# Gated attention kernel: another order of the first chunks' layers and loads, and separate buffers for x and attention

## Chip, core and metric

The kernel runs on one NeuronCore of a Trainium2 chip. The metric is the device time of one launch in microseconds (us), median of several runs. A profiled execution gives a span and a trace of every engine: TensorE (PE, matmuls; its weight loads are PEld), VectorE (DVE), ScalarE (ACT), GpSimd (POOL), and SyncE (SP), which only issues DMAs here.

## The reference

x and ctx are (4, 512, 512) in float32, H = 16 heads of HD = 32. What is computed:

```python
Q = layernorm(x) @ Wq.T + bq; K = ctx @ Wk.T + bk; V = ctx @ Wv.T + bv   # each as (b, s, 16, 32)
score = einsum('bshd,bsgd->bshg', Q, K)          # per token: 16 heads against 16 heads
attn = einsum('bshg,bsgd->bshd', softmax(score), V).reshape(b, s, 512)
x = x + tanh(g_xattn) * (attn @ Wo.T + bo)
x = x + tanh(g_ffn) * (layernorm(x) @ (Wf * scale[:, None]).T + bf)
```

The attention is inside a token: each token has a 16 x 16 matrix of scores between its heads.

## The kernel before, in words

The 2048 tokens are worked through in 8 chunks of 256 tokens (two tiles of 128). A chunk goes through these stages, named as in the text:

- **K, V** (from the chunk's context, loaded transposed by `load_ctx`), **Q** (from the normalised x, turned on TensorE by `turn_x1`): dense layers, 512 x 512.
- **score**: the queries and keys are brought to another layout by way of DRAM (`save_q`, `load_q`, `save_k`, `load_k`, then `lay_keys` on ScalarE), and 64 small matmuls give the scores, in two banks.
- softmax on VectorE (`scores_turn`, `softmax_a`, `softmax_b`) with the exponential on ScalarE (`exp`); then the weights are spread into a larger tile by VectorE (`spread_first`) and GpSimd (`spread_last`).
- **attend**: 64 small matmuls against V (reloaded by `load_v`), copied out by ScalarE (`attn_copy`).
- **O** (attention times Wo), residual, second layernorm, turning (`turn_x2`), **F** (times Wf), residual, output.

Every dense layer splits both operands into a high and a low part (float32r) and runs three products: high x high, high x low, low x high. High parts are made by ScalarE (`high`, line 541), low parts by VectorE (`low`, line 675), and for the context by GpSimd (`ctx_low`, line 927). This holds for the weights too, which are loaded and split piece by piece at the start (`load_w`, `w_high`, `w_low`; `W_ORDER` in line 180 sets the order that the counting semaphores `w_hi` and `w_lo` assume). K, Q, V and O, F share two PSUM banks, acc0 and acc1: a layer may write a bank when the layer before has been read out of it (`bank_free`). K and Q are written two 128-column blocks a bank ("block 0" and "block 1" are the banks).

Each engine has its own instruction stream, written out by hand. First a prologue (SP lines 303 to 332, TensorE 491 to 500, ScalarE 624 to 637, VectorE 811 to 830, GpSimd 953 to 972), then a step function that is called for chunk 0 and 1, in a hardware loop for 2 and on, and again for the last ones. An engine runs its stream strictly in order, and waits at semaphores for others. On TensorE a step i before is: score(i), O(i-1), K(i+1), Q(i+1), attend(i), turn x2(i-1), V(i+1), F(i-1), turn x1(i+2). In the prologue it is K0 with x0's turning in its middle, Q0, V0, turning of x1, and 6 warming matmuls (`keep_clock`, whose counts are in `WARM`).

Some orders matter in the prediction. The raw W_f and W_v are loaded into the tile `late`, into which `attn_copy` writes the attention as well, so the first copy waits for W_f's low parts (line 599). The raw W_k, W_q and W_o are loaded into the `spread` tile. In the prologue GpSimd runs root(0, 1), the inverse standard deviation of chunk 1's x, and behind it ctx_low(1). VectorE makes the statistics for it in norm_stats(0, x_norm, 1), line 823, and waits in `w_low` for the high part of the piece. The high parts of x1 and of the attention share the tile `xa_parts`. `tanh_g`, made by ScalarE in step 0, waits for all five constants (`consts_in`), as do VectorE's `scale_w` calls.

## Time and profile before

| | us |
|---|---|
| median of 3 runs | 323.98 (323.53 to 325.38) |
| profiled execution, its own time | 322.51 |
| its span | 320.8 |
| TensorE busy | 292.4 (91%) |
| VectorE busy | 216.5 (67%) |
| ScalarE busy | 141.3 (44%) |
| GpSimd busy | 107.3 (33%) |
| mean granted TensorE clock | 0.968 of full |

The chain of waits that ended last spends 61% of the span in TensorE, 13% in DMAs, 10% in VectorE and 8% in SyncE's queue. A row of a timeline gives the start in us from the span's start, the duration, the engine and source line, output and inputs by tile, and in brackets how long the engine had been idle and what released it. Rows of several instructions are merged, so that the duration holds small waits. The granted clock is 1.0 at 2.4 GHz and 0.5 at 1.2 GHz.

### The profile page before, as it was taken

To read this page: it belongs to the slowest core of one execution; us is meant where nothing else is said; L and a number is where in the kernel's file an instruction comes from. 1 tells how busy PE (TensorE), PEld (TensorE's weight loads), DVE (VectorE), ACT (ScalarE), POOL (GpSimd) and SP (SyncE) were. 2 spreads that over 40 slices of the span, in tenths; PEclk is the share of its full clock that TensorE was granted. 3 is DMA by queue.
4 is the path that set the end of the run, shared out by engine and by line. 5 is a ranking of instruction groups with operands and counts; after the bars stand their busy time and mean duration, and the time that the engine had idled before them with its cause. 6 is when DMAs were issued, how large, how long until landed. Compare 5 with 4: busy or idle time off the path is not lost.

```text
span 320.8 us, 6628 instructions
## 1 busy us (share of the span) xinstructions
PE 292.4 (91%) x2562; PEld 258.9 (81%) x2562; DVE 216.5 (67%) x321; ACT 141.3 (44%) x277; POOL 107.3 (33%) x83
## 2 busy tenths in 40 slices
PE   6499699759998999999999999999999997894895
PEld 6498699548986899889988898889988996774684
DVE  3857479835876696568774887568746953497463
ACT  4355424572377033923385236803592239304500
POOL 3500215520445133533173126214433342042422
PEclk9869899959999999999999999999999999799999
DMA  7966688473543735364543556184436226512001
GB/s 224 332 225 212 218 227 264 137 190 85 188 151 118 191 133 195 115 149 140 176 142 135 127 196 190 71 196 153 174 131 134 66 87 183 127 66 67 33 33 67
DMA packets 64596, 48.52 MB, mean 151 GB/s; under 512 B 35776, under 2 KB 53952, under 8 KB 64576
## 3 DMA queue, kind: packets, MB, share of 16 engines
q1 hardware_dynamic: 64576, 48.25, 49.0%
q8 instruction: 13, 0.21, 0.3%
q14 instruction: 7, 0.06, 0.1%
HBM read 31.46 MB, written 16.78 MB: 150 GB/s over the span
## 4 chain that ended last, share of the span: by engine, by line
PE 61%; DMA 13%; DVE 10%; SPq 8%; issue 4%; ACT 3%; POOL 1%; DVEq 0%; POOLq 0%
PE acc L377 48%; PE score_ps L463 6%; DMA k_scratch<-k_t 6%; PE turn_ps L406 4%; DMA q_scratch<-q_t 3%; PE attn_ps L478 3%; DVE spread L786 3%; SPq L230 2%; DMA x_norm<-x 2%; DMA q_pad<-q_scratch 2%; ACT late L602 2%; SPq L271 2%; DVE x_norm L711 2%; DVE stats L689 2%; SPq L256 1%
## 5 line engine op out<-in xcount | busy, mean ns | idle before, releaser
L602 ACT ACTIVATE late<-attn_ps 32x256 f32<-32x256 f32 x128 | 48.1, 376 | 24.9 <-PE attn_ps L478 18.2
L946 POOL TENSOR_TENSOR spread<-probs_t,same_token 128x1536 f32<-128x1536 f32 (+1 forms) x8 | 26.2, 3278 | 75.2 <-DVE probs_t L778 75.2
L377 PEld LDWEIGHTS acc<-ctx_parts,wk_parts 128*128 128x128 f32 x384 | 48.9, 199 | 1.9 <-issue 1.4
L377 PE MATMUL acc<-ctx_parts,wk_parts 128*128 128x256 f32 x384 | 49.6, 290 | 0.8 <-DVE wk_parts L675 0.8
L377 PE MATMUL acc<-wf_parts,x_parts 128*128 128x512 f32 (+1 forms) x192 | 44.7, 387 | 3.0 <-ACT x_parts L541 1.6
L377 PE MATMUL acc<-xa_parts,wq_parts 128*128 128x256 f32 x384 | 47.4, 283 | 0.0
L377 PE MATMUL acc<-wo_parts,xa_parts 128*128 128x512 f32 x192 | 46.1, 395 | 0.8 <-ACT xa_parts L541 0.8
L377 PEld LDWEIGHTS acc<-xa_parts,wq_parts 128*128 128x128 f32 x384 | 46.7, 192 | 0.0
L377 PE MATMUL acc<-wv_parts,ctx_parts 128*128 128x512 f32 x192 | 45.7, 393 | 0.0
L377 PEld LDWEIGHTS acc<-wo_parts,xa_parts 128*128 128x128 f32 x192 | 35.7, 189 | 10.2 <-issue 1.7
L377 PEld LDWEIGHTS acc<-wf_parts,x_parts 128*128 128x128 f32 x192 | 34.7, 188 | 11.1 <-ACT x_parts L541 2.4
L921 POOL TENSOR_TENSOR rstd<-var_eps,minus_half 128x1 f32<-128x1 f32 (+1 forms) x24 | 15.2, 634 | 85.0 <-DVE var_eps L700 85.0
L377 PEld LDWEIGHTS acc<-wv_parts,ctx_parts 128*128 128x128 f32 x192 | 35.5, 188 | 7.3 <-issue 0.2
L927 POOL TENSOR_TENSOR ctx_parts<-ctx_raw,ctx_parts 128x1024 fp32r<-128x1024 f32 (+1 forms) x8 | 18.7, 2340 | 44.7 <-ACT ctx_parts L541 44.7
L463 PE MATMUL score_ps<-q_pad,k_keys 128*32 128x128 f32 x512 | 23.3, 348 | 10.7 <-DMA q_pad<-q_scratch 7.5
L786 DVE TENSOR_TENSOR spread<-probs_t,same_token 128x2560 f32<-128x2560 f32 (+1 forms) x8 | 32.4, 4048 | 0.0
L463 PEld LDWEIGHTS score_ps<-q_pad,k_keys 128*32 128x32 f32 x512 | 19.7, 133 | 13.0 <-DMA q_pad<-q_scratch 7.9
L576 ACT ACTIVATE q_t<-acc,bq_col 128x256 f32<-128x256 f32 x32 | 13.5, 472 | 30.6 <-PE acc L377 30.5
L711 DVE TENSOR_SCALAR x_norm<-x_norm,moments,rstd 128x512 f32<-128x512 f32 x16 | 22.7, 1461 | 6.2 <-POOL rstd L921 6.2
L569 ACT ACTIVATE probs<-probs 128x512 f32<-128x512 f32 x8 | 5.1, 633 | 49.5 <-DVE probs L763 49.5
L576 ACT ACTIVATE k_t<-acc,bk_col 128x256 f32<-128x256 f32 x32 | 13.4, 471 | 28.4 <-PE acc L377 28.4
L748 DVE STREAM_TRANSPOSE turned<-score_ps 128x512 f32<-128x512 f32 x16 | 11.5, 719 | 20.1 <-PE score_ps L463 20.1
(62 smaller groups left out, 352.9 us busy)
## 6 DMA issues: line engine op xcount, KB each, us to landing
ctx_raw<-ctx_t SPq DMA_DIRECT2D x8, 512.0 KB, 4.4
x_norm<-x SPq DMA_DIRECT2D x8, 512.0 KB, 6.0
k_scratch<-k_t SPq DMA_DIRECT2D x8, 512.0 KB, 3.5
k_rows<-k_scratch SPq DMA_DIRECT2D x32, 128.0 KB, 2.9
q_scratch<-q_t SPq DMA_DIRECT2D x8, 512.0 KB, 3.4
q_pad<-q_scratch SPq DMA_DIRECT2D x32, 128.0 KB, 2.8
v_scratch<-v_or_norm SPq DMA_DIRECT2D x8, 512.0 KB, 2.8
v_keys<-v_scratch SPq DMA_DIRECT2D x8, 512.0 KB, 4.8
```

The source lines that it names most:

```text
L377: last = pe.matmul(dst, left(a, k), right(b, k), start=(n == 0), stop=(n == len(terms) - 1))
L406: last = pe.transpose(turn_ps[t][:, P * k:P * (k + 1)], src[:, t, P * k:P * (k + 1)], ident[:])
L463: last = pe.matmul(score_ps[b][HD * pair:HD * (pair + 1), P * o:P * (o + 1)], k_keys[:, 2 * n:2 * n + 2].rearrange("p s g -> p (s g)"), q_ ...
L478: last = pe.matmul(attn_ps[HD * t:HD * (t + 1), P * eight:P * (eight + 1)], v_keys[:, GT // OCT * t + eight, :], spread[:, GROUPS // TILES ...
L576: nc.scalar.activation(dst[:, :, m, :], acc[m // 2][:, TOK * (m % 2):TOK * (m % 2 + 1)].rearrange("p (t n) -> p t n", t=GROUPS), ACT.Ident ...
L602: nc.scalar.activation(attn_t[HD * q:HD * (q + 1), :, GT * t:GT * (t + 1)] .rearrange("p m (o e) -> p m o e", e=OCT), attn_ps[HD * t:HD * ...
L711: nc.vector.tensor_scalar(dst[:, t, :], src[:, t, :], moments[which][:, t, 0:1], rstd[which][:, t:t + 1], ALU.subtract, ALU.mult).then_inc ...
L748: nc.vector.transpose(flat[:, BANK * b:BANK * (b + 1)].rearrange("p (e s x) -> p e s x", s=2, x=HT), score_ps[b][:].rearrange("p (e x s) - ...
L786: nc.vector.tensor_tensor(spread[:, :n].rearrange("p o h t -> p (o h) t"), probs_t[:, :n].rearrange("p o h -> p (o h)").unsqueeze(2).broad ...
L921: nc.gpsimd.tensor_tensor(rstd[which][:, t], var_eps[which][:, t], minus_half[:, t], ALU.pow).then_inc(n_rstd[which], count)
L927: nc.gpsimd.tensor_tensor(ctx_parts[:, LO, k], ctx_raw[:, k], ctx_parts[:, HI, k].bitcast(F32), ALU.subtract).then_inc(ctx_lo, 1)
L946: nc.gpsimd.tensor_tensor(spread[:, first:].rearrange("p o h t -> p (o h) t"), probs_t[:, first:].rearrange("p o h -> p (o h)").unsqueeze( ...
```

## The change

The x parts and the attention parts get a tile each, `x1_parts` and `at_parts`, so that their writers wait for their own readers only. The order of layers on TensorE becomes K0, V0 (x0's turning in its middle), Q0, K1, turning of x1, block 0 of Q1; in step 0 score 0, block 1 of Q1, V1, attend 0; in step 1 score 1, K2, O0, Q2, attend 1 and on as before. From step 2 on it is the old order. The order of the weights becomes K, V, Q, O, F, and SyncE, ScalarE and VectorE follow the new order. GpSimd clears `q_pad` ahead of its first root and leaves all of context 0's low part to VectorE. First uses of a weight wait for its high part at the start of the product and for its low part only where it is read; the order of the mixed products is turned round where that postpones the wait. The 6 warming matmuls go.

```diff
-WARM = (12, 6, 0, 2, 4, 3)
+WARM = (12, 0, 2, 4, 3)
...
-        xa_parts = sb("xa_parts", [P, 2, KC, TOK], F32R)
+        x1_parts = sb("x1_parts", [P, 2, KC, TOK], F32R)
+        at_parts = sb("at_parts", [P, 2, KC, TOK], F32R)
...
-        W_ORDER = [("wk", wk_t, 0, (0, P, D // 2)), ("wq", wq_t, 1, (0, D // 2)), ("wv", wv_t, 2, (0, D // 2)),
+        W_ORDER = [("wk", wk_t, 0, (0, P, D // 2)), ("wv", wv_t, 2, (0, D // 2)), ("wq", wq_t, 1, (0, D // 2)),
                    ("wo", wo_t, 0, (0, D // 2)), ("wf", wf_t, 2, (0, D // 2))]
-        WK, WQ, WV, WO, WF = range(len(W_ORDER))
...
             load_ctx(0)
-            load_w(WK, 0)
-            load_w(WK, 1)
+            for j in range(3):
+                load_w(WK, j)
             load_x(0)
-            load_w(WK, 2)
+            for j in range(2):
+                load_w(WV, j)
             for col, dram in ((bk_col, bk), (bq_col, bq)):
                 sp.dma_start(col[:], dram).then_inc(biases_in, DMA)
-            for n in (WQ, WV):
-                for j in range(2):
-                    load_w(n, j)
             sp.dma_start(bv_row[:], bv.partition_broadcast(P)).then_inc(bv_in, DMA)
+            for j in range(2):
+                load_w(WQ, j)
+            load_ctx(1)
+            save_k(0)
             load_x(1)
-            load_ctx(1)
+            load_k(0)
             load_w(WO, 0)
+            save_v(0)
             load_w(WO, 1)
-            save_k(0)
-            load_k(0)
             save_q(0)
             sp.wait_ge(zeroed, 1)
             load_q(0)
-            save_v(0)
+            save_k(1)
+            load_v(0)
             load_w(WF, 0)
             load_w(WF, 1)
             sp.dma_start(scale_row[:], scale.partition_broadcast(P)).then_inc(consts_in, DMA)
             for n_gate, dram in enumerate((g_attn, g_ffn)):
                 sp.dma_start(gates[:, n_gate:n_gate + 1], dram.partition_broadcast(P)).then_inc(consts_in, DMA)
+            load_k(1)
             for row, dram in ((bo_row, bo), (bf_row, bf)):
...
                 if exists(i + 1):
-                    save_k(i + 1)
-                    load_k(i + 1)
+                    if not first(i):
+                        save_k(i + 1)
+                        load_k(i + 1)
                     save_q(i + 1)
                     load_q(i + 1)
                 if exists(i + 1):
...
-
-                terms = [(k, a, b) for a, b in ((HI, HI), (HI, LO), (LO, HI)) for k in range(KC)]
+            def product(dst, left, right, low_ready=None, right_low_ready=None, right_low_last=False):
+
+                mixed = ((LO, HI), (HI, LO)) if right_low_last else ((HI, LO), (LO, HI))
+                terms = [(k, a, b) for a, b in ((HI, HI), *mixed) for k in range(KC)]
                 for n, (k, a, b) in enumerate(terms):
                     if low_ready and (k, a) == (0, LO):
                         low_ready()
...
-                                (lambda: low_ready(t)) if low_ready and n == 0 else None).then_inc(done, 1)
-
-            def cols_layer(w, parts, done, prev, prev_c, w_new=None, between=None):
-
-                for b in range(2):
+                                (lambda: low_ready(t)) if low_ready and n == 0 else None,
+                                w_low_ready if t == 0 else None, bool(w_low_ready)).then_inc(done, 1)
+
+            def cols_layer(w, parts, done, prev, prev_c, w_new=None, low_ready=None, blocks=range(2)):
+
+                for b in blocks:
                     bank_free(prev, prev_c, b)
                     for m in (2 * b, 2 * b + 1):
-                        if between and m == 2:
-                            between()
+                        w_low_ready = None
                         if w_new is not None and P * m in W_ORDER[w_new][3]:
-                            pe.wait_ge(w_lo, pieces_to(w_new, W_ORDER[w_new][3].index(P * m)))
+                            ready = pieces_to(w_new, W_ORDER[w_new][3].index(P * m))
+                            pe.wait_ge(w_hi, ready)
+
+                            def w_low_ready(ready=ready):
+                                pe.wait_ge(w_lo, ready)
                         last = product(acc[b][:, TOK * (m % 2):TOK * (m % 2 + 1)],
                                        lambda a, k: weights[w][:, a, k, P * m:P * (m + 1)],
-                                       lambda c, k: parts[:, c, k, :])
+                                       lambda c, k: parts[:, c, k, :],
+                                       w_low_ready, low_ready if m == 0 else None)
                     last.then_inc(done, 1)
...
-                rows_layer(ctx_parts, "wv", v_mm, lambda t: bank_free("q", c, t))
-
-            def q_layer(c, w_new=None):
-                pe.wait_ge(x1_lo, TILES * (c + 1))
-                cols_layer("wq", xa_parts, q_mm, "k", c, w_new)
-
-            def k_layer(c, prev, prev_c, w_new=None, between=None):
-                pe.wait_ge(ctx_lo, c + 1)
-                cols_layer("wk", ctx_parts, k_mm, prev, prev_c, w_new, between)
+            def v_layer(c, prev="q", t_done=None):
+                def high_ready(t):
+                    if t_done and t == 1:
+                        t_done()
+                    bank_free(prev, c, t)
+                    if first(c) and t == 0:
+                        pe.wait_ge(w_hi, pieces_to(WV, 1))
+                rows_layer(ctx_parts, "wv", v_mm, high_ready,
+                           w_low_ready=(lambda: pe.wait_ge(w_lo, pieces_to(WV, 1))) if first(c) else None)
+
+            def q_layer(c, prev="k", prev_c=None, w_new=None, blocks=range(2)):
+                if 0 in blocks:
+                    pe.wait_ge(x1_lo, TILES * (c + 1))
+                cols_layer("wq", x1_parts, q_mm, prev, c if prev_c is None else prev_c, w_new, blocks=blocks)
+
+            def k_layer(c, prev, prev_c):
+                if first(c):
...
+                    cols_layer("wk", ctx_parts, k_mm, prev, prev_c)
             def o_layer(c, prev, prev_c):
                 def high_ready(t):
                     pe.wait_ge(at_hi, TILES * c + t + 1)
                     bank_free(prev, prev_c, t)
-                rows_layer(xa_parts, "wo", o_mm, high_ready, lambda t: pe.wait_ge(at_lo, TILES * c + t + 1))
+                rows_layer(at_parts, "wo", o_mm, high_ready, lambda t: pe.wait_ge(at_lo, TILES * c + t + 1))
...
             keep_clock(WARM[0])
-            pe.wait_ge(ctx0_lo, 1)
-            k_layer(0, None, 0, w_new=WK, between=lambda: turn_x1(0, lambda t: None))
-            q_layer(0, w_new=WQ)
-            pe.wait_ge(w_lo, pieces_to(WV, 1))
-            v_layer(0)
+            k_layer(0, None, 0)
+            v_layer(0, "k", lambda: turn_x1(0, lambda t: None))
+            q_layer(0, "v", 0, WQ)
+            k_layer(1, "q", 0)
             turn_x1(1, x1_read(0))
-
-            keep_clock(WARM[1])
+            q_layer(1, blocks=(0,))
             def tensor_step(i):
...
                     f_layer(i - 2, "v", i)
-                if exists(i - 1):
-                    if not exists(i - 2):
-                        pe.wait_ge(w_lo, pieces_to(WO, 1))
-                    o_layer(i - 1, *(("f", i - 2) if exists(i - 2) else ("v", i)))
-                if exists(i + 1):
-                    k_layer(i + 1, *(("o", i - 1) if exists(i - 1) else ("v", i)))
-                    q_layer(i + 1)
+                if first(i):
+                    q_layer(1, blocks=(1,))
+                    v_layer(1)
+                elif first(i - 1):
+                    k_layer(2, "v", 1)
+                    pe.wait_ge(w_lo, pieces_to(WO, 1))
+                    o_layer(0, "k", 2)
+                    q_layer(2, "o", 0)
+                else:
+                    if exists(i - 1):
+                        o_layer(i - 1, "f", i - 2)
+                    if exists(i + 1):
+                        k_layer(i + 1, "o", i - 1)
+                        q_layer(i + 1)
                 if exists(i):
                     attend(i)
...
                         f_layer(i - 1, "v", i + 1)
                 else:
+                    keep_clock(WARM[2 * (i - CHUNKS) + 3])
+                    turn_x2(i - 1, x2_read(i - 2), (0,))
                     keep_clock(WARM[2 * (i - CHUNKS) + 4])
-                    turn_x2(i - 1, x2_read(i - 2), (0,))
-                    keep_clock(WARM[2 * (i - CHUNKS) + 5])
                     f_layer(i - 1, "o", i - 1, lambda: turn_x2(i - 1, x2_read(i - 2), (1,)))
...
                 def free():
-                    if exists(c - 2):
-                        act.wait_ge(o_mm, TILES * (c - 1))
-                    else:
-                        reached(act, q_mm, 2 * c)
-                turned_hi(xa_parts, x1_turned, x1_hi, c, free)
+                    reached(act, q_mm, 2 * c)
+                turned_hi(x1_parts, x1_turned, x1_hi, c, free)
             def x2_high(c):
                 turned_hi(x2_parts, x2_turned, x2_hi, c, lambda: reached(act, f_mm, TILES * c))
...
                 if tile == 0:
-                    act.wait_ge(q_mm, 2 * (c + 2) if exists(c + 1) else 2 * CHUNKS)
+                    reached(act, o_mm, TILES * c)
                 act.wait_ge(a_out, MOVES * c + MOVES // TILES * (tile + 1))
-                high(xa_parts[:, HI, :, P * tile:P * (tile + 1)],
+                high(at_parts[:, HI, :, P * tile:P * (tile + 1)],
                      attn_t[:, :, P * tile:P * (tile + 1)]).then_inc(at_hi, 1)
             def w_high(n, j):
...
             ctx_high(0)
-            for n, j in ((WK, 0), (WK, 1), (WK, 2), (WQ, 0), (WQ, 1)):
+            for n, j in ((WK, 0), (WK, 1), (WK, 2), (WV, 0), (WV, 1)):
                 w_high(n, j)
+            act.wait_ge(biases_in, 2 * DMA)
+            k_bias(0, (0,))
+            w_high(WQ, 0)
+            k_bias(0, (1,))
+            w_high(WQ, 1)
             x1_high(0)
-            act.wait_ge(biases_in, 2 * DMA)
-            k_bias(0)
-            w_high(WV, 0)
-            w_high(WV, 1)
-            q_bias(0)
+            ctx_high(1)
+            q_bias(0, (0,))
             w_high(WO, 0)
+            q_bias(0, (1,))
             w_high(WO, 1)
-            ctx_high(1)
+            lay_keys(0)
+            k_bias(1)
             x1_high(1)
-            lay_keys(0)
+            q_bias(1, (0,))
             def scalar_step(i):
                 if exists(i):
                     exp(i)
-                if exists(i + 1):
-                    if not first(i):
-                        x1_high(i + 1)
+                if exists(i + 1) and not first(i):
+                    x1_high(i + 1)
                     k_bias(i + 1)
                 if first(i):
                     act.wait_ge(consts_in, 5 * DMA)
                     nc.scalar.activation(tanh_g[:], gates[:], ACT.Tanh).then_inc(gates_done, 1)
-                if exists(i + 1):
-                    q_bias(i + 1)
                 if first(i):
+                    q_bias(1, (1,))
+                    lay_keys(1)
                     w_high(WF, 0)
                     w_high(WF, 1)
+                elif exists(i + 1):
+                    q_bias(i + 1)
                 if exists(i):
                     attn_copy(i, 0)
                 if exists(i - 1):
                     x2_high(i - 1)
+                if first(i):
+                    attn_high(i, 0)
                 if exists(i):
                     attn_copy(i, 1)
-                if exists(i + 1):
+                if exists(i + 1) and not first(i):
                     lay_keys(i + 1)
                 if exists(i):
-                    attn_high(i, 0)
+                    if not first(i):
+                        attn_high(i, 0)
                     attn_high(i, 1)
                 if exists(i + 2):
                     ctx_high(i + 2)
...
             dve.wait_ge(ctx_hi, 1)
-            low(ctx_parts[:, LO, :KC // 2], ctx_raw[:, :KC // 2], ctx_parts[:, HI, :KC // 2]).then_inc(ctx0_lo, 1)
-            w_low(WK, 0)
-            w_low(WK, 1)
+            low(ctx_parts[:, LO], ctx_raw[:], ctx_parts[:, HI]).then_inc(ctx_lo, 1)
+            for j in range(3):
+                w_low(WK, j)
             norm_stats(0, x_norm, 0)
-            norm_apply(0, x_norm, x_norm, 0)
-            w_low(WK, 2)
-            w_low(WQ, 0)
-            turned_lo(xa_parts, x1_hi, x1_lo, 0)
-            w_low(WQ, 1)
             w_low(WV, 0)
             w_low(WV, 1)
+            norm_apply(0, x_norm, x_norm, 0)
+            w_low(WQ, 0)
+            dve.wait_ge(bv_in, DMA)
+            v_bias(0, 0)
+            w_low(WQ, 1)
+            turned_lo(x1_parts, x1_hi, x1_lo, 0)
+            v_bias(0, 1)
+            w_low(WO, 0)
             norm_stats(0, x_norm, 1)
             norm_apply(0, x_norm, x_norm, 1)
-            dve.wait_ge(bv_in, DMA)
-            v_bias(0, 0)
-            w_low(WO, 0)
             w_low(WO, 1)
-            v_bias(0, 1)
-            turned_lo(xa_parts, x1_hi, x1_lo, 1)
+            turned_lo(x1_parts, x1_hi, x1_lo, 1)
             def vector_step(i):
                 if final(i - 1):
                     return last_step(i)
                 scores_turn(i)
-                if first(i - 1):
-                    o_residual(i - 1, 0)
                 softmax_a(i)
                 if final(i):
                     return last_softmax_step(i)
-                if first(i - 1):
-                    o_residual(i - 1, 1)
-                elif exists(i - 1):
+                if exists(i - 1) and not first(i - 1):
                     o_residual(i - 1, 0)
                 softmax_b(i)
                 if exists(i - 1) and not first(i - 1):
                     o_residual(i - 1, 1)
                 if exists(i + 1) and not first(i):
-                    turned_lo(xa_parts, x1_hi, x1_lo, i + 1)
+                    turned_lo(x1_parts, x1_hi, x1_lo, i + 1)
                 spread_first(i)
+                if first(i - 1):
+                    o_residual(i - 1, 0)
+                    o_residual(i - 1, 1)
                 if first(i):
                     dve.wait_ge(consts_in, 5 * DMA)
                     scale_w(0)
...
             nc.gpsimd.affine_select(out=same_token[:], in_=same_token[:], compare_op=ALU.is_ge, fill=0.0,
                                     base=H - 1, pattern=[[H, OCT]], channel_multiplier=-1).then_inc(consts_made, 1)
-            ctx_low(0, KC // 2)
+            nc.gpsimd.memset(q_pad[:], 0.0).then_inc(zeroed, 1)
             root(0, 0)
-            nc.gpsimd.memset(q_pad[:], 0.0).then_inc(zeroed, 1)
             root(0, 1)
             ctx_low(1)
             pool.wait_ge(w_lo, pieces_to(WO, 1))
```

## Rows read from the trace of the kernel before

**Rows 1.** Windows (stretch, length, busy per engine, clock, DMA share, GB/s): a loop step.

```profile
104.55:138.89 34.34, 34.34 (x315) 30.55 (x313) 24.25 (x38) 16.23 (x33) 10.81 (x10) 1.00 0.48 149
```

**Rows 2.** The chain that ended last (start, us, what).

```profile
17.28 4.55 PE acc L377 x24
...
22.78 4.92 DMA k_scratch<-k_t
...
105.42 2.46 PE score_ps L463 x60
107.88 17.18 PE acc L377 x120
```

**Rows 3.** Timeline of TensorE: start, duration, operation, idle before and its releaser.

```profile
15.31 1.97 PE L406 MATMUL turn_ps<-ident,x_norm 128*128 128x128 f32 x8 [4.28 <-DVE x_norm L711]
...
27.41 5.63 PE L377 MATMUL acc<-wv_parts,ctx_parts 128*128 128x512 f32 x24
...
37.81 3.55 PE L463 MATMUL score_ps<-q_pad,k_keys 128*32 128x128 f32 x64 [2.55 <-DMA q_pad<-q_scratch]
...
68.06 3.64 PE L463 MATMUL score_ps<-q_pad,k_keys 128*32 128x128 f32 x64 [4.97 <-DMA q_pad<-q_scratch]
71.63 5.99 PE L377 MATMUL acc<-wo_parts,xa_parts 128*128 128x512 f32 x24
...
98.84 5.71 PE L377 MATMUL acc<-wf_parts,x_parts 128*128 128x512 f32 x24 [1.34 <-DVE v_or_norm L742]
```

**Rows 4.** Timeline of VectorE, 0 to 60 us.

```profile
25.95 1.28 DVE L689 BATCH_NORM_STATS2 stats<-x_norm 128x6 f32<-128x512 f32 x2
...
41.41 0.72 DVE L748 STREAM_TRANSPOSE turned<-score_ps 128x512 f32<-128x512 f32 x1 [0.99 <-PE score_ps L463]
...
49.60 5.01 DVE L727 TENSOR_TENSOR late<-late,scale_row 128x1024 f32<-128x1024 f32 x2
...
57.19 2.35 DVE L675 TENSOR_TENSOR wf_parts<-late,wf_parts 128x1024 fp32r<-128x1024 f32 x2
```

**Rows 5.** Timeline of ScalarE, 0 to 70 us.

```profile
11.51 1.06 ACT L541 ACTIVATE wq_parts<-spread 128x1024 fp32r<-128x1024 f32 x1 [0.42 <-DMA spread<-wq_t]
12.87 1.06 ACT L541 ACTIVATE wq_parts<-spread 128x1024 fp32r<-128x1024 f32 x1 [0.31 <-DMA spread<-wq_t]
...
21.85 0.84 ACT L576 ACTIVATE k_t<-acc,bk_col 128x256 f32<-128x256 f32 x2 [3.21 <-PE acc L377]
...
59.63 6.37 ACT L602 ACTIVATE late<-attn_ps 32x256 f32<-32x256 f32 x16 [3.74 <-DVE wf_parts L675]
66.03 1.93 ACT L590 ACTIVATE k_keys<-k_rows 128x1024 f32<-128x1024 f32 x1
```

**Rows 6.** Timeline of GpSimd, 0 to 75 us.

```profile
28.05 0.70 POOL L921 TENSOR_TENSOR rstd<-var_eps,minus_half 128x2 f32<-128x2 f32 x1 [13.07 <-DVE var_eps L700]
...
70.06 2.39 POOL L927 TENSOR_TENSOR ctx_parts<-ctx_raw,ctx_parts 128x1024 fp32r<-128x1024 f32 x1 [7.97 <-ACT ctx_parts L541]
```

**Rows 7.** The page's DMA issues: count, size of one, median us to landing.

```profile
ctx_raw<-ctx_t SPq DMA_DIRECT2D x8, 512.0 KB, 4.4
...
k_scratch<-k_t SPq DMA_DIRECT2D x8, 512.0 KB, 3.5
...
spread<-wo_t SPq DMA_DIRECT2D x2, 512.0 KB, 6.9
```

**Rows 8.** Timeline of SyncE: issues and how long each held it.

```profile
27.78 1.76 SPq L271 DMA_DIRECT2D k_rows<-k_scratch  x4
...
41.17 7.26 SPq L230 DMA_DIRECT2D x_norm<-x  x1
...
69.10 3.48 SPq L230 DMA_DIRECT2D x_norm<-x  x1
```

**Rows 9.** Windows of one us; the clock stands third from the end.

```profile
20.00:21.00 1.00, 1.00 (x7) 1.00 (x6) 0.31 (x1) 0.00 (x0) 0.00 (x0) 0.52 1.02 363
...
72.00:73.00 1.00, 1.00 (x5) 0.79 (x5) 0.47 (x1) 0.00 (x0) 0.45 (x1) 0.92 0.62 97
```

39 lines of the change are left out of this document (20 added, 19 removed).

## The prediction

> **What bounds the kernel now.** I read the stretches of the windows first: from the third chunk on TensorE is busy for 34.34 of each 34.34 us at full granted clock [rows 1], so a change that leaves the loop's work alone can only gain or lose ahead of it. The chain that ended last says the same: the layers of a loop step follow each other without a gap, three of them in 17.18 us (5.73 each) and the scores in 2.46 [rows 2]. The change moves nothing across the loop's start: by the loop's first score both kernels have done the same matmuls but for 6 warming ones. What counts is therefore at what time the last layer ahead of the loop, F of chunk 0, starts. Before, that is 98.84 us, after a 1.34 us wait [rows 3].
>
> Then I asked what set TensorE's pace up to there. It waits 2.55 us for the padded queries before score 0 (37.81), 4.97 us before score 1 (68.06), and runs from O0 (71.63) to the end of V2 (98.84 - 1.34 = 97.50) practically without a stop, 25.87 us [rows 3]. Behind score 0 lies a chain outside TensorE, which is the backbone of what follows: VectorE's last transpose of score 0 starts at 41.41, its low parts of W_f end at 59.54 (57.19 + 2.35) [rows 4]; ScalarE's copies of attention 0 wait for just that (59.63 to 66.00), then it lays the keys of chunk 1 (1.93) [rows 5]; at last GpSimd makes the low part of context 2, ending at 72.45 [rows 6]. From 41.41 to 72.45 are 31.04 us, and K2 needs its end. Before, O0 stands ahead of K2 and covers the last of it.
>
> **The change, part by part, in order of time.**
>
> *K0, V0, Q0.* K0 needs the high part of W_k first and its low part later, so it runs behind the loads. The second piece of W_v stands in the load order where the second piece of W_q stood, and that was converted from 12.87 on [rows 5]: V's high part is there at 13.9, the first half of K0's bias (0.84) at 14.8. V0 with x's turning (5.73 and about 1) ends at 21.5, Q0 at 27.3. Before, Q0 and V0 together were done at 33.0 [rows 3]. The clearing of q_pad, moved ahead of GpSimd's first root, costs nothing, since GpSimd waits there for VectorE. That is a lead of some 5 us, and the question is who takes it back.
>
> *K1.* K1 waits for context 1's low part. On GpSimd this stands behind the root of chunk 1's x (`root(0, 1)`, then `ctx_low(1)`); the root waits for VectorE's statistics of chunk 1; and the new order of VectorE puts these behind the low part of W_o's first piece. That piece is loaded by a queue entry that was moved behind the saving and reloading of K0. Before, it was issued before K was saved, and the statistics stood ahead of it. So a layer of chunk 1 now hangs on a weight of the O layer. The chain:
> - W_q's first piece: 512 + 512 + 256 KB more stand ahead of it than before, at 1.36 us per 512 KB (11.51 to 12.87) [rows 5], 3.4 us: 14.9. High part 1.06, second half of K0's bias 0.84 [rows 5]: 16.8.
> - K0's saving. It took 4.92 with more in the queue [rows 2]; a 512 KB load has a median of 4.4 [rows 7], K's saving one of 3.5. I take 4.4, ends 3.5 and 4.92: 21.2.
> - Four reloads are issued in 1.76 [rows 8]: 23.0.
> - W_o's first piece: median 4.4 for a context load, 6.9 for W_o before, where all came at once [rows 7]. Few bytes stand ahead of it now, so 4.4: 27.5.
> - High 1.06, low 1.18 (half of 2.35) [rows 4, 5]: 29.7.
> - Statistics up to the root's start, 25.95 to 28.05, and the root, 0.70 [rows 4, 6]: 32.5.
> - Low part of context 1, 2.39 [rows 6]: 35.0 with the gaps.
>
> So K1 starts at 35.0 instead of 27.3: TensorE stands for 7.7 us. For the last item, GpSimd and VectorE are released by the same root. The rows have GpSimd starting its next instruction at once after a root, so I take 2.39 undelayed. The Trainium skill (SBUF — State Buffer, "SBUF: two separate sides") says that the two share one port pair as an exclusive lock and that the first to start holds it; if the normalising of x came first, context 1 would be up to 1.0 us later, and so would the sum.
>
> *The clock.* Before, after waits of 4.28, 2.55 and 4.97 us TensorE came back at 1.2 GHz: from 15.31 to 21.0, from 37.81 to 41.4 and from 68.06 to 72.1 [rows 3, 9]. The granted clock is 0.52 in the 21st us, and 0.92 in the 73rd, so full from 72.2. The half of K0 that ran at 1.2 GHz for 3.7 of its us took 4.55 instead of 2.87, which is 0.45 us lost per us [rows 2]. K1 after 7.7 us of waiting then loses 4.1 x 0.45 = 1.85, ends 1.6 and 2.6. The Trainium skill (TensorE: Matmul & The Clock Gate, "Terms") puts the loss at half the slow time; that would be 2.05, and the sum 0.4 higher for two layers. The waits of some 2 us before V0 and before Q1 I cost at nothing, nearest to the 1.34 one [rows 3] after which no slow stretch followed; 1.85 each if wrong.
>
> *Up to score 0.* K1 ends at 35.0 + 5.73 + 1.85 = 42.6. Second half of its bias 0.84, high part of x 1.06 (as many values as W_q's piece), low part of its second half 0.6 (half of 1.18), 0.3 of gaps [rows 4, 5]: 45.4. Half of Q1, 2.87: score 0 starts at 48.3 and ends at 50.8, its queries having long landed. VectorE's last transpose starts at 50.8 instead of 41.41: 9.4 us late.
>
> *The backbone.* Its work is unchanged but that the keys of chunk 1 are laid earlier, out of it: 31.04 - 1.93 = 29.1. K2 can start at 50.8 + 29.1 = 79.9. The second half of Q1, V1, attend 0 and the turning fill only part of it; these 11 or 12 us cover nothing that ends later. Score 1 runs in the gap, some 7 us ahead of that, and a gap of 3.7 us is left, so K2 too starts at 1.2 GHz: 1.85, low end 0. Then K2, O0, Q2, attend 1, turning, V2: 25.87 less the 0.2 that O0 lost before, plus 1.85, gives 107.4 for F0's start. Its own wait of 1.34 goes, because O0's residuals, which it hung on, come earlier relative to V2.
>
> *The rest.* Own buffers for x1 and attention let ScalarE take x's high part earlier in each step; TensorE has no gap there that could shrink [rows 1]: nothing. The later order of the product's terms changes no count: nothing. Loads of V, W_f and constants now stand behind K1's saving. The next issue after the V reload was held for 7.26 or 3.48 us [rows 8]. From 43.5 with 3.5 I get the last constant issued at 52.3 and landed by 58 to 60; VectorE wants it at 59: nothing, 4 if the hold is 7.3.
>
> **Sum.** 107.4 - 98.84 = 8.6 us. The profiled execution took 322.51 us, so 331.1; it lies 1.5 below the median of the runs, 323.98, to which I add the same: 332.6, forecast 332.5. Low ends (saving 0.9 less, clock 0.25 and 1.85 less, some 3 in all): 329.5. High ends (W_o 2.5 more, saving 0.5, clock 0.8 twice, port 1.0): 338.
>
> **Rivals.**
> - *K1 doesn't wait.* W_o's piece would have to be there 7.5 us before 27.3, at 19.8. By the rows K0's save is not even back then. If so all the same, score 0 ends near 41.7, K2 can start near 71.0, and F0 starts at 98.5 if K2 is slow, 96.7 if not: 323.6 or 321.8. The second is faster by 0.7%, and decides from K2's clock. For it: every other part of the change takes a wait away. Together 0.14, 0.07 of each.
> - *The constants bind.* If the V reload holds the queue for the 7.26 of before, bo and bf land near 63, W_f's scaling starts 4 us late, and all of it reaches K2: 336.5. Against it: the 7.26 came with W_f and the constants queued ahead, which they aren't now. 0.12.
> - *The backbone is shorter.* The scaling of W_f took 5.01 us for two pieces whose low parts took 2.35 [rows 4], GpSimd's share of the spread beside it. Without that the backbone would lose 2.7: 329.8. Against it: the spread stays on both engines. 0.10.
> - *A smaller wait at K1 that the chain takes up, other small gains:* 324 to 326, 0.04.
>
> **How the numbers follow.** My forecast has 0.60. Rows carry each link, but the start is made of many. The range from 325.5 to 337.5 takes in the forecast's ends but for the last 0.5, the constants and the shorter backbone; left out are the first rival and the far tails, some 0.17. About 0.5% (1.6 us) is what a measurement of this kernel can tell from no change. Slower 0.84 (forecast, constants, backbone and half the last), same 0.09 (the first rival with a slow K2, and half the last), faster 0.07 (the first rival with a fast K2).
>
> **What would show it.** K1's first matmul should start at 34 to 37 us, released by GpSimd's low part of context 1, which follows the root directly; W_o's high part should be released by its DMA at 27 to 28. The granted clock should be at 1.2 GHz in K1. Score 0 ends near 51, VectorE's low W_f near 69, K2 starts near 80 released by GpSimd, with 3 to 4 us of wait, and F0 near 107 with none. The loop's period should stay at 34.34. If K1 starts before 30, the forecast is wrong at its root; if K1 is late and K2 isn't, the backbone was not what I took it for.

## The result, and the profile after

The changed kernel is slower: 334.11 us median of 4 runs (333.88 to 337.1) against 324.68 of the kernel before, a ratio of 1.034 (95% interval 1.027 to 1.041), and the medians lie 9.4 us apart. Ratios and intervals, here and below, are taken from the runs outside a slower state in which some executions fall, so they are not the quotients of the medians, which here would be 1.029. The profiled execution took 334.08 us with a span of 332.3.

From the page after (busy time and share of the span; K's layer with its idle time and what ended it):

```profile
PE 294.8 (89%) x2550; PEld 259.8 (78%) x2550; DVE 214.1 (64%) x321; ACT 141.5 (43%) x277; POOL 106.3 (32%) x82
...
L381 PE MATMUL acc<-ctx_parts,wk_parts 128*128 128x256 f32 x384 | 52.6, 300 | 13.5 <-POOL ctx_parts L956 13.1
```

TensorE's work is the same, 294.8 us against 292.4. K's layers waited 13.5 us, 13.1 of them for GpSimd's low parts of the context, a wait that the page before doesn't have. The chain that ended last (start, us, what) shows the first of these waits from its source:

```profile
17.21 2.99 DMA k_scratch<-k_t
...
20.27 0.34 SPq L269
...
22.08 6.28 DMA spread<-wo_t
28.38 1.06 ACT wo_parts L567
29.47 1.23 DVE wo_parts L707
30.69 1.21 DVE stats L721 x2
...
32.69 0.70 POOL rstd L951
33.39 2.32 POOL ctx_parts L956
...
35.75 7.56 PE acc L381 x48
...
54.00 7.38 DMA bf_row<-bf
...
78.65 2.35 POOL ctx_parts L956
...
81.05 19.85 PE acc L381 x120
```

K0's saving starts at 17.21 and its reloads at 20.27. Only then, at 22.08, is W_o's first piece asked for. From there one thing follows the other: high part, low part, statistics of chunk 1, root, low part of context 1, K1 at 35.75. The constants (54.00), and behind them the low part of context 2 (78.65), lead to K2 at 81.05. Between VectorE's low parts of W_f and that last low part stands ScalarE, with the copies of attention 0 and the high part of context 2, which GpSimd waited for:

```profile
69.89 3.16 ACT L626 ACTIVATE late<-attn_ps 32x256 f32<-32x256 f32 x8 [3.73 <-DVE wf_parts L707]
...
77.53 1.04 ACT L567 ACTIVATE ctx_parts<-ctx_raw 128x1024 fp32r<-128x1024 f32 x1
```

TensorE's timeline, with the idle time ahead of a group and its releaser:

```profile
20.99 5.91 PE L381 MATMUL acc<-x_parts,wq_parts 128*128 128x256 f32 x48
35.75 7.55 PE L381 MATMUL acc<-ctx_parts,wk_parts 128*128 128x256 f32 x48 [8.86 <-POOL ctx_parts L956]
...
46.04 3.13 PE L381 MATMUL acc<-x_parts,wq_parts 128*128 128x256 f32 x24 [1.87 <-DVE x_parts L707]
49.11 2.52 PE L484 MATMUL score_ps<-q_pad,k_keys 128*32 128x128 f32 x64
...
81.05 8.63 PE L381 MATMUL acc<-ctx_parts,wk_parts 128*128 128x256 f32 x48 [4.21 <-POOL ctx_parts L956]
...
109.11 5.61 PE L381 MATMUL acc<-wf_parts,x_parts 128*128 128x512 f32 x24
```

Q0 ends at 26.9, where before V0 ended at 33.0 [rows 3]: the lead of 6 us is there. K1 then waits 8.86 us and score 0 starts at 49.11 instead of 37.81. K2 waits 4.21 us, and F0 starts at 109.11 instead of 98.84, 10.27 us later. VectorE's rows for the same stretch:

```profile
33.43 3.01 DVE L743 TENSOR_SCALAR x_norm<-x_norm,moments,rstd 128x512 f32<-128x512 f32 x2 [0.88 <-POOL rstd L951]
...
51.69 0.72 DVE L780 STREAM_TRANSPOSE turned<-score_ps 128x512 f32<-128x512 f32 x1 [0.43 <-PE score_ps L484]
...
61.40 3.46 DVE L759 TENSOR_TENSOR late<-late,scale_row 128x1024 f32<-128x1024 f32 x2 [1.45 <-DMA bf_row<-bf]
...
67.45 2.35 DVE L707 TENSOR_TENSOR wf_parts<-late,wf_parts 128x1024 fp32r<-128x1024 f32 x2
```

The clock, in stretches of the changed kernel (granted clock third from the end), beside a loop step:

```profile
39.00:40.00 1.00, 1.00 (x9) 1.00 (x9) 0.00 (x0) 0.00 (x0) 0.00 (x0) 0.88 0.00 0
81.00:87.00 6.00, 5.96 (x28) 5.96 (x29) 5.20 (x9) 2.09 (x4) 2.07 (x1) 0.50 0.28 91
306.00:308.00 2.00, 1.96 (x5) 1.57 (x6) 1.15 (x2) 0.00 (x0) 0.99 (x2) 0.50 0.00 0
114.56:148.90 34.34, 34.34 (x314) 30.55 (x313) 24.26 (x39) 16.24 (x33) 12.41 (x9) 1.00 0.51 154
```

K1 runs at 1.2 GHz until 39.2, K2 until 87, and the loop step takes its 34.34 us as before [rows 1]. Of the 11.5 us between the spans, 10.27 are there when F0 starts. The other 1.2 come in the last chunk: here the clock was low from 306 to 308.9, and the first product of an F layer took 3.43 us where it had been 2.11 before:

```profile
306.04 3.43 PE L381 MATMUL acc<-wf_parts,x_parts 128*128 128x512 f32 x8 [1.64 <-ACT x_parts L567]
```

This is scatter and no effect of the change: after a wait of 1.62 to 1.64 us the same product took 3.68 to 3.78 us in the traces of experiments 6, 8 and 9, and 2.11 or 2.12 in those of the other seven.

### The profile page after: what moved, and what is told of

Same layout as the page of the kernel before. It is cut to its first block, busy times and chain, and to the rows that moved or that the text cites. A ratio compares the mean times of both kernels' runs of the same rounds, so it can differ in the third digit from the quotient of the medians.

```text
span 332.3 us, 6598 instructions
## 1 busy us (share of the span) xinstructions
PE 294.8 (89%) x2550; PEld 259.8 (78%) x2550; DVE 214.1 (64%) x321; ACT 141.5 (43%) x277; POOL 106.3 (32%) x82
## 4 chain that ended last, share of the span: by engine, by line
PE 70%; DMA 7%; DVE 6%; SPq 5%; issue 5%; POOL 3%; ACT 3%; DVEq 0%; POOLq 0%
PE acc L381 57%; PE score_ps L484 5%; PE attn_ps L499 4%; PE turn_ps L415 3%; SPq L299 2%; DMA spread<-wq_t 2%; DMA bf_row<-bf 2%; DMA spread<-wo_t 2%; ACT late L626 2%; POOL ctx_parts L956 1%; DVE stats L721 1%; DVE spread L818 1%; DVE late L759 1%; POOL rstd L951 1%; SPq L269 1%
## 5 line engine op out<-in xcount | busy, mean ns | idle before, releaser
L381 PE MATMUL acc<-ctx_parts,wk_parts 128*128 128x256 f32 x384 | 52.6, 300 | 13.5 <-POOL ctx_parts L956 13.1
L381 PE MATMUL acc<-wv_parts,ctx_parts 128*128 128x512 f32 x192 | 48.2, 406 | 6.2 <-ACT q_t L600 4.9
L381 PE MATMUL acc<-x_parts,wq_parts 128*128 128x256 f32 x384 | 47.7, 283 | 1.9 <-DVE x_parts L707 1.9
L381 PEld LDWEIGHTS acc<-x_parts,wq_parts 128*128 128x128 f32 x384 | 46.8, 192 | 2.5 <-DVE x_parts L707 2.1
L381 PE MATMUL acc<-wo_parts,at_parts 128*128 128x512 f32 x192 | 45.7, 394 | 0.9 <-ACT at_parts L567 0.9
L381 PEld LDWEIGHTS acc<-wo_parts,at_parts 128*128 128x128 f32 x192 | 35.5, 188 | 9.8 <-issue 1.3
L707 DVE TENSOR_TENSOR x_parts<-turn_ps,x_parts 128x512 fp32r<-128x512 f32 x32 | 20.7, 682 | 21.7 <-ACT x_parts L567 21.7
L956 POOL TENSOR_TENSOR ctx_parts<-ctx_raw,ctx_parts 128x1024 fp32r<-128x1024 f32 x7 | 17.0, 2428 | 36.5 <-ACT ctx_parts L567 36.5
L707 DVE TENSOR_TENSOR at_parts<-late,at_parts 128x512 fp32r<-128x512 f32 x16 | 10.5, 688 | 20.9 <-ACT at_parts L567 20.9
L567 ACT ACTIVATE x_parts<-turn_ps 128x512 fp32r<-128x512 f32 x32 | 17.6, 597 | 14.4 <-PE turn_ps L415 14.1
```

Of the source, the lines that this page charges most:

```text
L381: last = pe.matmul(dst, left(a, k), right(b, k), start=(n == 0), stop=(n == len(terms) - 1))
L567: return nc.scalar.activation(dst, src, ACT.Identity)
L707: return nc.vector.tensor_tensor(dst, src, hi.bitcast(F32), ALU.subtract)
L956: nc.gpsimd.tensor_tensor(ctx_parts[:, LO], ctx_raw[:], ctx_parts[:, HI].bitcast(F32), ALU.subtract).then_inc(ctx_lo, 1)
```

## The experiments

In all of them "before" is the kernel before, run on the same chip between them: 322.7 us median for experiments 1, 2, 3 and 5, 323.6 for 4, 6, 7 and 8, 323.0 for 9 and 10. Ratios are to that. A trace shows one execution, and its own time is given where it lies far from the median. The order of V0 and Q0, the later waits for low parts and the missing warming matmuls were not run by themselves.

**1. GpSimd makes context 1's low part ahead of the root.**

```diff
-            root(0, 1)
             ctx_low(1)
+            root(0, 1)
```

> The changed kernel, but GpSimd makes the low part of context 1 ahead of the root of chunk 1's x. Theory (K1 hangs on W_o's first piece by way of that root): context 1's low part is done by 25, K1 starts at 27 with no wait worth naming, its second half at 30.2, score 0 ends near 42.7 instead of 51.5, all behind it moves by the same 8.8 us, so K2 starts near 72.3, F0 near 100.4, and the time is 325.3 against 334.1. Rival (K1's wait was idle time that the chain behind score 0 would have taken anyway, through the constants or the copies of attention): K1 starts at 27 too, but K2 stays after 77 and the time above 330.

Measured: 326.01 us, ratio 1.014 (1.007 to 1.021). TensorE:

```profile
26.31 3.04 PE L381 MATMUL acc<-ctx_parts,wk_parts 128*128 128x256 f32 x24
...
71.63 8.05 PE L381 MATMUL acc<-ctx_parts,wk_parts 128*128 128x256 f32 x48 [4.29 <-POOL ctx_parts L956]
...
99.12 5.61 PE L381 MATMUL acc<-wf_parts,x_parts 128*128 128x512 f32 x24
```

One line gives back 10.0 us of F0's start in the trace and 2% of the time. (The profiled execution took 322.86 us, the least of the four, which go up to 328.19.) K1 starts at 26.31 with no wait; its second half waits 0.22 for ScalarE. The expected 72.3 for K2 and 100.4 for F0 came out at 71.63 and 99.12. K2 still waits 4.29 us. So the wait of K1 is the larger part of the loss, and it isn't slack that the chain behind score 0 would have used.

**2. VectorE makes chunk 1's statistics ahead of W_o's low part.**

```diff
-            w_low(WO, 0)
             norm_stats(0, x_norm, 1)
             norm_apply(0, x_norm, x_norm, 1)
+            w_low(WO, 0)
```

> The changed kernel, but VectorE makes chunk 1's statistics and norm ahead of the low part of W_o's first piece; GpSimd keeps its order. Theory (the link from W_o to the statistics is what delays the root): x of chunk 1 lands near 22.2, root by 25.0, context 1's low part by 27.4, K1 starts at 27.4, and the time is within 0.5 us of the kernel with the context ahead of the root, near 325.5. Rival (it is GpSimd's own order or context 1's high part that delays it, not W_o): K1 starts after 33, and the time stays near 334.

Measured: 325.84 us, 1.013 (1.006 to 1.019); the profiled execution took 323.62.

```profile
27.05 6.02 PE L381 MATMUL acc<-ctx_parts,wk_parts 128*128 128x256 f32 x48 [0.18 <-POOL ctx_parts L956]
...
99.81 5.61 PE L381 MATMUL acc<-wf_parts,x_parts 128*128 128x512 f32 x24
```

The other end of the same link, with the same effect: GpSimd's order alone does no harm if the root isn't kept waiting by W_o. Each cut of the link is enough.

**3. Warming matmuls in the two waits.**

```diff
+            keep_clock(66)
             k_layer(1, "q", 0)
...
+                    pe.wait_ge(v_out, TILES + 1)
+                    keep_clock(30, acc[0])
                     k_layer(2, "v", 1)
```

> The changed kernel with 66 warming matmuls ahead of K1 and 30 ahead of K2 (these into acc0, once V1 has been read out of it), so that neither wait is idle; nothing else moves. Theory (K1 and K2 lose to the 1.2 GHz clock after their waits): K1 takes 5.8 instead of 7.55 us, score 0 ends 1.8 earlier, and so does K2's start; K2 takes 5.8 to 6.0 instead of 8.63, so 2.7 more: 329.6 against 334.1. Rival (the slow layers are covered by the chain outside TensorE, as the queries' reload or the constants): under 1.5 us of gain, above 332.5.

Measured: 336.91 us, 1.047 (1.041 to 1.052), slower than the changed kernel.

```profile
26.80 14.90 PE L510 MATMUL score_ps<-ident 128*128 128x128 f32 x132
41.46 6.00 PE L381 MATMUL acc<-ctx_parts,wk_parts 128*128 128x256 f32 x48
...
88.72 6.00 PE L381 MATMUL acc<-ctx_parts,wk_parts 128*128 128x256 f32 x48
```

A miss, by my counting: the warming matmuls are two instructions each, and 66 take 14.90 us, not 8.3. They held K1 until 41.46 and K2 until 88.72. But both K layers took 6.00 us, near the 5.92 of K in the loop, instead of 7.55 and 8.63. So this run shows the price of the clock, but not what it costs the kernel; for that the fillers have to fit the waits.

**4. The same with 36 and 16.**

```diff
-            keep_clock(66)
+            keep_clock(36)
...
-                    keep_clock(30, acc[0])
+                    keep_clock(16, acc[0])
```

> As the last kernel with warming matmuls, but 36 ahead of K1 and 16 ahead of K2, because one of them takes 0.226 us (14.90 us for 66) and not the 0.125 that I had counted. Theory (the slow clock in K1 and K2 is on the path): K1 still starts at 35.8 and takes 6.0, score 0 ends 1.6 earlier than in the changed kernel, K2 takes 6.0 instead of 8.63, F0 starts 4.2 earlier, near 104.9; 1.021 of the kernel before. Rival (covered by the queue's or VectorE's chain): F0 after 107.5, 1.03 or more.

Measured: 329.61 us, 1.017 (1.009 to 1.026).

```profile
37.03 6.00 PE L381 MATMUL acc<-ctx_parts,wk_parts 128*128 128x256 f32 x48 [0.55 <-POOL ctx_parts L959]
...
80.82 6.02 PE L381 MATMUL acc<-ctx_parts,wk_parts 128*128 128x256 f32 x48 [0.37 <-POOL ctx_parts L959]
...
106.27 5.61 PE L381 MATMUL acc<-wf_parts,x_parts 128*128 128x512 f32 x24
```

The waits stay and only the clock is kept up: K1 and K2 take 6.0 us. In this execution W_o's first piece was asked for 1.4 us later (23.48), so that K1 starts at 37.03, 1.3 later, and F0 at 106.27 instead of the expected 104.9. By the ratios about half of the loss is given back. Between the two traces the spans differ by 4.1 us: 2.8 up to F0, and 1.3 in the last chunk's product, which took 2.12 us here and is scatter. Both layers' slow clock is on the path.

**5. Own buffers alone, in the kernel before.** The x parts and the attention parts get a tile each, and their writers wait only for Q and for O.

```diff
-                    if exists(c - 2):
-                        act.wait_ge(o_mm, TILES * (c - 1))
-                    else:
-                        reached(act, q_mm, 2 * c)
-                turned_hi(xa_parts, x1_turned, x1_hi, c, free)
+                    reached(act, q_mm, 2 * c)
+                turned_hi(x1_parts, x1_turned, x1_hi, c, free)
...
-                    act.wait_ge(q_mm, 2 * (c + 2) if exists(c + 1) else 2 * CHUNKS)
+                    reached(act, o_mm, TILES * c)
```

> The kernel before with one part of the change alone: own buffers for the x parts and the attention parts, and the waits that go with them. Theory (TensorE has no gap in the loop that could shrink): no difference beyond 0.3%, 322.5 to 325.5, loop period 34.34. Rival (the separate buffers free a wait before the loop or in the last chunks): faster by 1 us or more.

Measured: 323.34 us (10 runs), 1.004 (0.999 to 1.008). No difference that can be told from none, and none over 0.8%; the loop's period is 34.34. In this trace score 0 waited 4.07 us for its queries, where it had been 2.55 before, and F0 started at 100.05; whether the edit has a part in that, one trace can't tell.

**6. Context 1 ahead of the root, and O0 ahead of K2 again.** On VectorE the residuals of O0 go back to their places around `softmax_a`.

```diff
-                    k_layer(2, "v", 1)
                     pe.wait_ge(w_lo, pieces_to(WO, 1))
-                    o_layer(0, "k", 2)
-                    q_layer(2, "o", 0)
+                    o_layer(0, "v", 1)
+                    k_layer(2, "o", 0)
+                    q_layer(2)
```

> The changed kernel with context 1's low part ahead of the root, and in step 1 O0 ahead of K2 as before the change (with its residuals placed on VectorE as before). Theory (K2 put ahead of O0 uncovers the wait for context 2, so the second loss sits there): score 1 ends near 67.4 and O0 starts at once on attention that is there at 64 and 69; K2 follows with no wait at full clock; Q2 ends near 84.7 instead of 90.8, then VectorE's chain lets F0 start near 94.7 instead of 99.1; 4.4 us faster than with the context alone, 0.99 to 0.995 of the kernel before. Rival (O0 waits as long for the attention as K2 for the context): F0 stays at 98 to 100.

Measured: 322.21 us (10 runs), 0.993 (0.988 to 0.999): 0.7% faster than the kernel before, and 2 points below experiment 1 (1.014). The profiled execution took 324.31.

```profile
71.11 5.71 PE L381 MATMUL acc<-wo_parts,at_parts 128*128 128x512 f32 x24
76.66 5.92 PE L381 MATMUL acc<-ctx_parts,wk_parts 128*128 128x256 f32 x48
...
98.09 5.73 PE L381 MATMUL acc<-wf_parts,x_parts 128*128 128x512 f32 x24 [1.39 <-DVE v_or_norm L774]
```

O0 follows score 1 with no wait and K2 follows O0 at full clock. So the second loss of the changed kernel is its order of K2 and O0. F0 at 98.09 missed the expected 94.7, because score 0 started at 43.35 instead of 39.66 as in experiment 1: this execution's K1 began 1.8 later, and its Q1 half, at 1.2 GHz, took 4.51 instead of 3.13. From score 0 to F0 it is 54.7 us, against 59.5 in experiment 1: 4.7 us gained, where 4.4 were expected.

**7. O0 ahead of K2 alone:** the changed kernel with the diff of experiment 6, TensorE's and VectorE's, and without that of experiment 1.

> The changed kernel with O0 ahead of K2 alone; K1's wait for the root stays. Theory (the two losses are separate and add up): K1 starts at 35.8 as in the changed kernel, K2 no longer waits, F0 starts near 103.5 instead of 109.1, 5.6 us faster than the changed kernel, 1.017 of the kernel before. Rival (the order of O0 and K2 matters only once K1 is early): F0 after 107.5, 1.03.

Measured: 329.48 us, 1.019 (1.011 to 1.028).

```profile
35.72 8.40 PE L381 MATMUL acc<-ctx_parts,wk_parts 128*128 128x256 f32 x48 [8.67 <-POOL ctx_parts L957]
...
79.30 5.73 PE L381 MATMUL acc<-wo_parts,at_parts 128*128 128x512 f32 x24
...
106.30 5.73 PE L381 MATMUL acc<-wf_parts,x_parts 128*128 128x512 f32 x24 [1.38 <-DVE v_or_norm L774]
```

K1 waits as in the changed kernel, the wait ahead of K2 is gone. F0 missed the expected 103.5 by 2.8 us, again ahead of score 0, which started at 51.38 instead of 49.11: K1 ran at 1.2 GHz until 41.2 and took 8.40, and Q1's half took 4.60. Behind score 0 the gain is 5.1 us, as the theory has it (5.6). From 1.034 this mends 1.5 points and experiment 1 mends 2.0; together (experiment 6) 4.1. Within the intervals the two add up.

**8. Three more mends.** Experiment 6 with the statistics of experiment 2, `lay_keys(0)` behind `x1_high(1)` on ScalarE, and on SyncE the loads of W_f and all constants ahead of `load_k(1)` and `load_v(0)`.

```diff
-            lay_keys(0)
             k_bias(1)
             x1_high(1)
+            lay_keys(0)
...
             save_k(1)
-            load_v(0)
             load_w(WF, 0)
...
-            load_k(1)
             for row, dram in ((bo_row, bo), (bf_row, bf)):
                 sp.dma_start(row[:], dram.partition_broadcast(P)).then_inc(consts_in, DMA)
+            load_k(1)
+            load_v(0)
```

> The kernel with context 1 ahead of the root and O0 ahead of K2, and three things more: chunk 1's statistics ahead of W_o's low part, the laying of chunk 0's keys behind K1's bias and x1's high part, and the loads of W_f and all constants ahead of the reloads of K1 and V0. Expected: score 0 starts near 38.3, the constants land by 47 so that neither the tanh nor the second half of V1 waits, VectorE's low W_f ends near 57.8, F0 starts near 91; 3.5 us faster than the kernel with the first two, 0.98 of the kernel before. Rival (VectorE's chain from score 0 on binds by itself, whatever the loads do): F0 at 94 or later.

Measured: 320.1 us, 0.987 (0.978 to 0.996), 1.3% faster than the kernel before; its interval overlaps that of experiment 6, so what the three add isn't shown by the times.

```profile
35.62 4.28 PE L381 MATMUL acc<-x_parts,wq_parts 128*128 128x256 f32 x24 [1.86 <-DVE x_parts L707]
...
68.15 5.75 PE L381 MATMUL acc<-wo_parts,at_parts 128*128 128x512 f32 x24
...
95.14 5.70 PE L381 MATMUL acc<-wf_parts,x_parts 128*128 128x512 f32 x24 [1.36 <-DVE v_or_norm L774]
```

Score 0 starts at 39.84, not at 38.3: again Q1's half fell to 1.2 GHz (4.28 us). F0 starts at 95.14, not at 91, after 1.36 us of waiting for VectorE; nobody waits for the constants any more, but W_f's low parts end at 60.77 instead of the expected 57.8. The rival that I had named holds: from score 0 on the chain that ended last runs through VectorE and through layers that wait for it, and from score 0 to F0 it is 55.3 us, no less than in experiment 6. Against the kernel before, score 0 starts 2.0 us later and F0 3.7 earlier: there score 1 waited 4.97 us for its queries and started at 68.06 [rows 3], here it starts at 64.69 without that wait.

**9. With 7 warming matmuls ahead of Q1's first half.**

```diff
+            keep_clock(7)
             q_layer(1, blocks=(0,))
```

> The mended kernel with 7 warming matmuls (1.58 us) in the 1.87 us wait ahead of Q1's first half. In the mended kernel that half took 4.28 instead of 3.13 us, at 1.2 GHz, in the changed kernel 3.13 after the same wait. Theory (waits of 2 us sometimes let the clock fall, and this one is on the path to score 0): Q1's first half takes 3.1 in the profile, score 0 ends by 41.5, F0 starts near 94, 1 us faster than the mended kernel, 0.983 of the kernel before. Rival (the clock falls there from the same activity whatever fills 1.6 us): no difference.

Measured: 319.97 us (12 runs), 0.987 (0.983 to 0.991); the profiled execution took 322.03.

```profile
64.62 3.64 PE L484 MATMUL score_ps<-q_pad,k_keys 128*32 128x128 f32 x64 [1.21 <-DMA q_pad<-q_scratch]
68.19 6.85 PE L381 MATMUL acc<-wo_parts,at_parts 128*128 128x512 f32 x24
```

The half took 3.14 us and score 0 ended at 41.2, as expected, but F0 started at 96.31 and not near 94, and the ratio didn't move. The rival's outcome, though not its reason: the 1.1 us gained before score 0 were lost again before O0, where score 1 waited 1.21 us for its queries (O0 starts at 68.19, in experiment 8 at 68.15), and O0 began at the low clock and took 1.1 us more.

**10. The mended kernel with the changed kernel's order of these loads:** the second half of experiment 8's diff is undone.

> The mended kernel with the changed kernel's order of the loads of W_f, the constants and the reloads of K1 and V0. Theory (the late constants stop ScalarE's tanh and the second half of V1, but hardly VectorE, so they aren't on the path): the constants land near 51, V1's second half waits 3 us or more, VectorE waits under 0.5, F0 within 0.5 of the mended kernel's 95.1, ratio 0.987. Rival (the constants are on the path): F0 at 96.5 or later, 0.992.

Measured: 318.47 us (12 runs), 0.988 (0.984 to 0.993), not to be told from experiment 8; the profiled execution took 317.33. V1's second half on TensorE, then F0:

```profile
53.78 5.49 PE L381 MATMUL acc<-wv_parts,ctx_parts 128*128 128x512 f32 x12 [5.22 <-ACT q_t L600]
...
94.48 5.71 PE L381 MATMUL acc<-wf_parts,x_parts 128*128 128x512 f32 x24 [1.44 <-DVE v_or_norm L774]
```

The scaling of W_f on VectorE:

```profile
52.79 3.19 DVE L759 TENSOR_TENSOR late<-late,scale_row 128x1024 f32<-128x1024 f32 x2 [1.72 <-DMA bf_row<-bf]
```

From the chain that ended last (start, us, what), the last constant and the first copy of attention 0:

```profile
46.23 6.55 DMA bf_row<-bf
...
61.35 0.37 ACT late L626
```

V1 waits 5.22 us for ScalarE. VectorE waits 1.72 us for the constants, where I had expected under 0.5, and F0 starts at 94.48. The rival (96.5 or later) is out, but "not on the path" says too much. The chain runs from the constants through V1's second half and attend 0 to ScalarE's copies at 61.35. Without the constants these would have waited for W_f's low parts until 60.91, so by this trace the late constants cost under 0.5 us, too little for the times to show.

## Why the prediction was right

It said 332.5 us, range 325.5 to 337.5, slower; measured were 334.11. The mechanism held: K1 hung on W_o's first piece by the chain that I had named, and K2's wait came where it was forecast. The steps against the trace after:

- *W_q's first piece* 14.9, found 15.34. *K0's saving* 4.4, found 2.99, below the low end of 3.5. *W_o's first piece* 4.4, found 6.28, between the ends. The last two errors nearly cancel, which is luck: the chain came to K1 at 35.75 instead of 35.0. Experiments 1 and 2 cut it in two places, each with the forecast effect.
- *GpSimd goes first after the root.* It did: the context's low part started at 33.39 and took 2.32, and VectorE's norm, released with it at 33.43, took 3.01 us. In experiment 2 the two met again, and it took 3.07. In experiment 1, where GpSimd had nothing to do there, it took 1.00 for the same two instructions:

```profile
32.80 1.00 DVE L743 TENSOR_SCALAR x_norm<-x_norm,moments,rstd 128x512 f32<-128x512 f32 x2 [0.88 <-POOL rstd L951]
```

  The Trainium skill's rule of the exclusive port pair (SBUF — State Buffer, "SBUF: two separate sides") agrees with this, the first to start being GpSimd.
- *K1's clock* 1.85, found 1.55 (7.55 against the 6.00 of experiment 3, counted alike): 3.5 us were slow and not 4.1. In experiment 7, the same up to there, it was 2.40. *K2's* 1.85, found 2.67 (19.85 for K2, O0 and Q2 against 17.18 [rows 2]): its first 6 us were slow. This term was mis-sized by 0.8. Both fit the 0.45 us per us that K0 had shown. Half the slow time, as the Trainium skill has it (TensorE: Matmul & The Clock Gate, "Terms"), would be 1.75 and 3.0; the measured losses lie a little below. Experiments 3 and 4 removed both.
- *The waits of some 2 us at nothing.* In this trace that held: V0 waited 1.25 us and Q1 1.87, and no slow stretch followed. But the reason I gave was none: 2 us is nearer to the 2.55 of score 0, after which the clock was low, than to 1.34. In experiments 6, 7 and 8 the clock was low after such a wait. It came out right by luck.
- *Score 0*'s last transpose started 0.9 later than forecast, 0.75 of it from K1's start. *The backbone* took 29.3 us (51.69 to 80.99), forecast 29.1. K2 started at 81.05, forecast 79.9.
- *The constants* landed at 61.38, later than the 58 to 60 that I gave (SyncE was held for 4.91 us at W_f's loads, not 3.5), and VectorE waited 1.45 for them. It cost nothing all the same: the scaling of W_f then took 3.46 instead of 5.01, with less of it beside GpSimd's share of the spread, which ended at 62.66. I had priced late constants at their full delay, and a shorter scaling as a gain of its own. The traces tie the two together: from the last transpose of score 0 to the end of W_f's low parts it is 18.1 us in all twelve, with waits for the constants from 0 to 1.72.
- *F0* at 109.11, forecast 107.4. The last 1.2 us, a low clock in the last chunk, stood in no step. Why the clock falls there in some executions was not tried.
- *The sum.* Between the two profiled executions lie 11.6 us, where my sum has 8.6: 1.7 are missing at F0 and 1.2 in the last chunk. That the forecast is only 1.6 us from the median is in part luck: I had added 1.5 because the profiled execution before lay that far below its median, and the one after lies on its own.
- *Own buffers:* nothing forecast, nothing found beyond the interval (experiment 5).

The rival that K1 wouldn't wait shows what it was worth: experiment 1 is that kernel, and F0 started at 99.12 in it, where I had 98.5 with a slow K2; K2 was slow. I had put its time at that of the kernel before, 323.6 us; it took 1.014 of it. The trace accounts for little of that: its F0 is 0.3 us later than before the change. The three runs that weren't profiled had a mean granted clock of 0.957 to 0.963 against its 0.973, and what they lost stands in no trace. Even with K1 mended the change isn't faster; with K2's order mended too, it is (experiment 6). My own step "25.87 from O0 to V2" took that order as given; that putting O0 back would bring 1.5 to 2% I found only by experiments 6 and 7.

## What to carry to other kernels

When a stream is reordered, follow each semaphore through every engine's program order: here a layer waited for the weight of another because a root, a statistic and a low part stood in line behind it on two engines, and one line moved mends it. Work that is brought forward gains only if the work left behind still covers the next wait; K2 ahead of O0 took the cover off a chain that nobody had shortened. A wait can cost twice, once as idle time and again as slow matmuls behind it: those of 8.86 and 4.21 us ahead of K1 and K2 did.

## What the runs showed of the hardware beyond that

A wait of 1.9 to 3.1 us ahead of Q1's first half sometimes cost 1.2 to 1.5 us of clock and sometimes nothing: that half took 3.13 us in the changed kernel and in experiments 1, 2, 4 and 10, but 4.51, 4.60 and 4.28 in 6, 7 and 8, after waits of 1.9 to 2.1. No run shows what decides.

More of the scatter between executions lies at the end. In the traces of experiments 8 and 10 F0 starts 0.7 us apart, but the spans are 4.1 apart (319.6 and 315.5). The rest is a low clock after the loop, in layers that both kernels have alike: the scores of the last chunk took 3.64 us against 2.48, the F layer behind them 6.83 against 5.76, and the first product of the next F layer 3.68 against 2.12. The 12 runs of experiment 10 alone go from 317.2 us, at a mean granted clock of 0.989, to 321.2 at 0.968. So differences of a few us between single executions say little here, and where a layer starts in a trace says more than the execution's time.
